# One tile fewer held as stored count blocks in passes 2 and 3 of a four-layer graph network kernel

## The chip, the cores and the metric

One NeuronCore of one Trainium2 chip runs the whole program. The metric is device time in microseconds (us) of one execution, the median of several runs.

## What is computed

A graph of 6250 nodes with 256 features and 106,250 directed edges (sources `src`, targets `dst`, sorted by target) goes through four layers, each followed by a residual sum and a layer norm. Cut to what matters here:

```python
# L0: weighted neighbour sums, two 256x256 products, row normalisation
# L1: three GIN layers on the unweighted graph:
agg = segment_sum(h[src], dst)            # the neighbour sum of each node
z = (1.0 + eps) * h + agg
h = relu(layer_norm(relu(z @ W1 + b1) @ W2 + b2 + h, gamma, beta))
# L2: degree-scaled neighbour sum, residual product, top-2 mixture of 64 experts, batch norm
# L3: weighted neighbour sums, one product
```

## The kernel before, in words

**Passes.** The nodes are 49 tiles of 128. Each of six neighbour sums is a *pass* over all 49 target tiles: pass 0 is L0, passes 1 to 3 are the GIN layers, pass 4 the sum of L2, pass 5 that of L3; the experts stand between passes 4 and 5. A pass's inputs are the outputs of the pass before, so little overlaps across its border.

**Two ways to sum.** In passes 1 to 4 a target tile is either *gathered* (sparse) or *held* (dense).
- A gathered tile has 18 chunks of 128 edges. For each chunk GpSimd issues one indirect DMA that fetches 128 rows of 512 floats, a value's high and low part (L2498), VectorE builds a 128x128 selection matrix (L3259), and TensorE multiplies the two (L2573, in pass 1 two halves at L2577).
- A held tile has 49 count blocks, 128x128 matrices of edge counts for each source tile, stored as bytes in `dense_blocks`. SyncE loads them in 7 parts (L2320), ScalarE widens them to float in 14 parts (L3085), and TensorE multiplies each with the source tile's rows that lie in SBUF (L2604, in pass 1 L2607).

**Building.** The blocks of 25 tiles (`DENSE`) are built in pass 0. Those of the tiles in `LATE` are built in pass 1, while it runs, for use from pass 2 on: for each of 13 places of a tile ScalarE and VectorE make one-hots (L3050, L3052, L3377), TensorE multiplies them (L2629), ScalarE copies the counts out as bytes (L3007) and SyncE stores them (L2268). Building needs the tile's edges sorted by source tile (`sort_into_bins`, VectorE L3282 to L3338). The other 24 tiles' edges are sorted too, for later passes: 14 in pass 1, one every 10 steps, and 10 in pass 3, one every 11 steps. With two tiles in `LATE`, passes 2 and 3 hold 27 tiles and gather 22. Pass 4 holds `DENSE` and one tile of `LATE`: 26 held and 23 gathered.

**Steps.** Every engine's program is written out at build time as a loop over steps `g`; six steps are one gathered tile, so a step is three chunks. `GROUPS[k]` is the number of gather steps of pass k: 144 in pass 1, 132 in passes 2 and 3, 138 in pass 4. The held tiles' blocks are spread evenly over the first `DSTEPS[k]` steps (120 in passes 2 and 3, 126 in pass 4), except that the first 28 blocks (`HEAD`) of a pass are multiplied at the end of the pass before. `_sequence` sets at which step each tile's sum is complete; the tile's layer work (operand, transposes, products, norm, split into parts, store) follows at fixed offsets from that step, on all engines (`OFFSETS`). Each engine works its program in order, so a late tile holds what stands behind it. GpSimd may run four steps ahead of TensorE (`RING`), VectorE's selection matrices two.

**Other work tied to steps.** In pass 2 a histogram of the edges' sources is taken, 49 parts, one every two steps from step 4 (`ONES_AT`): VectorE builds two large one-hot arrays (`one_hot`, L3451 to L3454) and TensorE multiplies them two steps later (`histogram`, L2707). A part's one-hots wait for the multiplication of the part before.

The change itself touches only the list at L1376; all schedules are computed from it.

Of the kernel before, what the change touches and what calls it, by code (L numbers as in the profile page):

```python
# [1372 lines left out]
DENSE_PASSES = (1, 2, 3, 4)  # L1373
WEIGHTED = {0: DENSE[1::3], 5: sorted(DENSE[1::2] + DENSE[4::8])}
EARLY_SPARSE = [t for t in range(NT) if t not in DENSE]
LATE = EARLY_SPARSE[6::12]  # L1376
LATE4 = LATE[:1]
HELD_IN = {1: DENSE, 2: sorted(DENSE + LATE), 3: sorted(DENSE + LATE), 4: sorted(DENSE + LATE4)}
STORED_AT = {t: i for i, t in enumerate(DENSE + LATE)}
NS = len(STORED_AT)  # L1380
# [10 lines left out]
SHORT = {0: 0, 1: 2, 2: 4, 3: 5, 4: 6, 5: 7, 6: 9, 8: 10, 9: 11}  # L1391
UNHELD = [t for t in EARLY_SPARSE if t not in LATE]
SORT_LATER = [t for pair in zip(LATE, UNHELD) for t in pair] + UNHELD[len(LATE):]
assert sorted(SORT_LATER) == EARLY_SPARSE
BINNED = [(0, t) for t in DENSE] + [(1 if j < SORTED1 else 3, t) for j, t in enumerate(SORT_LATER)]
BIN_AT = [APART * i for i in range(ND)] + [3 + SORT_APART[1] * i for i in range(SORTED1)] + [3 + SORT_APART[3] * i for i in range(NT - ND - SORTED1)]
BUILT = [(0, t) for t in DENSE] + [(1, t) for t in LATE] + [(5, t) for t in WEIGHTED[5]]
BIN_OF = [BINNED.index(b) if b in BINNED else None for b in BUILT]
# [2510 lines left out]
```

## Time and profile before

| | |
|---|---|
| runs | 5572.49, 5583.52 and 5602.99 us; median 5583.52 |
| span of the profiled execution, first to last instruction | 4918.0 us |
| what lies around the span, against the median | 665.5 us |
| mean granted TensorE clock | 0.947 |
| busy | TensorE 91%, VectorE 77%, GpSimd 65%, ScalarE 54% |

The profiled execution's own total is not listed, only its span; the difference to the median of the runs is what lies before the first and after the last instruction, and the spread between executions. "Busy" of TensorE is modelled from starts and contains short waits; VectorE's comes from recorded ends. A number like 4.26 us per step is worked out from the gathers counted in a window, three to a step.

### The profile page before, as it was taken

What the parts mean: (1) busy time and instruction counts of PE and PEld (TensorE: products, weight loads), DVE (VectorE), ACT (ScalarE), POOL (GpSimd) and SP (SyncE); (2) the same over time, 40 slices, a digit from 0 to 9 for tenths busy, and PEclk for the clock granted to TensorE, in tenths of its full rate; (3) what the DMA queues carried; (4) which work ended last, traced back from release to release, by engine and by line L of the source; (5) the groups of instructions that cost most, each with busy time, mean ns of one, the idle gap of its engine ahead of it and who ended that gap; (6) DMA issues with size and microseconds to landing.
All of it is one profiled execution on the core that took longest, in us unless ns stands there. A gap on an engine that the chain in (4) does not pass through costs nothing.

```text
span 4918.0 us, 84668 instructions
## 1 busy us (share of the span) xinstructions
PE 4481.9 (91%) x25759; PEld 3786.5 (77%) x25759; DVE 3796.1 (77%) x12081; ACT 2670.8 (54%) x6497; POOL 3216.8 (65%) x3227
## 2 busy tenths in 40 slices
PE   6999888889998899989999699996999877999998
PEld 4777777779997788857777488885999745888887
DVE  7888888759998799858988556667989457777776
ACT  4888888837553444535555344443555413454553
POOL 6777777767776666667666577672455363777776
PEclk9999999989999999989999899996999968999999
DMA  6444444488889888898888988885677533444443
GB/s 173 133 137 129 129 138 130 142 283 278 273 271 315 259 252 252 252 315 277 265 252 263 318 262 258 257 250 163 228 249 234 178 90 111 113 114 113 113 113 96
DMA packets 542065, 1005.46 MB, mean 204 GB/s; under 512 B 104266, under 2 KB 318920, under 8 KB 541324
## 3 DMA queue, kind: packets, MB, share of 16 engines
q0 software_dynamic: 206976, 637.24, 43.4%
q1 hardware_dynamic: 317354, 346.98, 21.6%
q10 hardware_dynamic: 17280, 15.74, 0.9%
q8 instruction: 217, 3.56, 0.3%
q14 instruction: 238, 1.95, 0.1%
HBM read 883.85 MB, written 117.06 MB: 204 GB/s over the span
## 4 chain that ended last, share of the span: by engine, by line
PE 43%; POOL 8%; issue 6%; DVE 5%; DMA 4%; ACT 1%; SPq 0%; ACTq 0%; POOLq 0%; DVEq 0%
PE PS L2604 15%; POOL ring L2498 5%; PE PS L2573 4%; PE PS L2862 4%; PE PS L2871 4%; PE PS L2756 4%; PE PS L2691 3%; PE PS L2580 2%; POOL more L2498 2%; PE PS L2741 1%; DMA ring<-expert_outputs,ring 1%; POOL slot_rows L2498 1%; PE PS L2730 1%; PE PS L2880 1%; POOL ring L2527 1%
## 5 line engine op out<-in xcount | busy, mean ns | idle before, releaser
L2498 POOL DMA_INDIRECT slot_rows<-planes,REC x1638 | 1580.3, 965 | 660.9 <-issue 433.6
L3085 ACT ACTIVATE wide_blocks<-HH 128x512 fp32r<-128x512 uint8 (+1 forms) x1470 | 831.7, 576 | 842.6 <-PE PS L2604 655.7
L2604 PE MATMUL PS<-plane_rows,wide_blocks 128*128 128x512 f32 x3920 | 1028.4, 409 | 17.2 <-ACT wide_blocks L3085 14.1
L2604 PEld LDWEIGHTS PS<-plane_rows,wide_blocks 128*128 128x128 f32 x3920 | 730.4, 192 | 173.3 <-ACT wide_blocks L3085 17.4
L2498 POOL DMA_INDIRECT ring<-in_x,REC x555 | 537.8, 969 | 210.8 <-issue 154.9
L2580 PE MATMUL PS<-ring,pick 128*128 128x256 f32 x2028 | 550.0, 404 | 60.2 <-DMA ring<-in_x,REC 32.6
L2498 POOL DMA_INDIRECT ring<-table,REC x459 | 442.7, 964 | 217.7 <-issue 208.5
L2691 PE MATMUL PS<-HH 128*128 128x256 f32 x2254 | 536.3, 379 | 0.0
L2580 PEld LDWEIGHTS PS<-ring,pick 128*128 128x128 f32 x2028 | 382.7, 200 | 158.1 <-DMA ring<-in_x,REC 48.8
L2691 PEld LDWEIGHTS PS<-HH 128*128 128x128 f32 x2254 | 413.9, 190 | 49.1
L2518 POOL DMA_INDIRECT ring<-second_outputs,ring x120 | 230.3, 1919 | 317.3 <-PE PS L2852 246.6
L3380 DVE TENSOR_SCALAR last_pass_pairs<-HH 128x256 fp32r<-128x256 f32 x780 | 278.1, 418 | 179.6 <-PE PS L2655 168.1
L2573 PE MATMUL PS<-slot_rows,slot_picks 128*128 128x512 f32 x1206 | 370.3, 410 | 49.2 <-DMA slot_rows<-planes,REC 46.8
L3259 DVE TENSOR_SCALAR slot_picks<-iotab,REC 128x128 fp32r<-128x128 bf16 x1638 | 376.5, 300 | 40.0 <-PE PS L2573 30.3
L2607 PE MATMUL PS<-plane_rows,wide_blocks 128*128 128x256 f32 (+1 forms) x2450 | 331.5, 289 | 6.0 <-DVE plane_rows L3668 6.0
L3257 DVE TENSOR_SCALAR pick<-iotab,REC 128x128 f32<-128x128 bf16 x1014 | 294.0, 352 | 41.8 <-PE PS L2580 39.1
L2573 PEld LDWEIGHTS PS<-slot_rows,slot_picks 128*128 128x128 f32 x1206 | 230.9, 192 | 123.2 <-DMA slot_rows<-planes,REC 45.5
L3050 ACT ACTIVATE last_pass_pairs<-iota,HH 128x128 fp32r<-128x128 f32 x390 | 135.1, 394 | 329.5 <-PE PS L2655 292.5
L2607 PEld LDWEIGHTS PS<-plane_rows,wide_blocks 128*128 128x128 f32 x2450 | 306.9, 192 | 8.0 <-DVE plane_rows L3668 6.2
L2966 ACT ACTIVATE TZT<-PS 128x256 f32<-128x256 f32 (+1 forms) x294 | 131.7, 448 | 250.0 <-PE PS L2730 248.3
L2756 PE MATMUL PS<-WA,TZT 128*128 128x256 f32 x980 | 247.3, 393 | 3.8 <-ACT TZT L2966 3.8
L2629 PE MATMUL PS<-HH 128*128 128x256 bf16 (+2 forms) x1075 | 223.1, 322 | 25.3 <-ACT HH L3011 19.8
(392 smaller groups left out, 9186.5 us busy)
## 6 DMA issues: line engine op xcount, KB each, us to landing
HH<-dense_blocks SPq DMA_DIRECT2D x735, 112.0 KB
HH<-in_L_gnn_w SPq DMA_DIRECT2D x128, 512.0 KB, 5.8
planes<-HN SPq DMA_DIRECT2D x188, 256.0 KB
plane_rows<-planes SPq DMA_DIRECT2D x57, 768.0 KB, 8.9
slot_rows<-planes,REC POOLq DMA_INDIRECT x1638
dense_blocks<-HH SPq DMA_DIRECT2D x25, 784.0 KB
expert_outputs<-ring ACTq DMA_DIRECT2D x120, 128.0 KB
ring<-in_x,REC POOLq DMA_INDIRECT x555
```

The source lines that it names most:

```text
L2498: pool.indirect_dma_start(to, None, planes[k] if dense else tables[k], bass.IndirectOffsetOnAxis(ap=at_rows, axis=0)).then_inc(s_slot[slot ...
L2518: pool.indirect_dma_start(XSB[c % MB], None, x2_dram, bass.IndirectOffsetOnAxis(ap=IDXC[:, c:c + 1], axis=0)).then_inc(s_xl[c % MB], 16)
L2573: last = mm(bank(j % 2, RP), slot_pick(k, slot), slot_row(k, slot, 0, RP), start=c == 0, stop=c == WT - 1)
L2580: last = mm(bank(j % 2, D), slot_pick(k, slot), slot_row(k, slot, 0, D), start=c == 0, stop=c == WT - 1)
L2604: last = mm(bank(5 + n % 2, RP), WIDE[:, at_block:at_block + P], plane(0, t, RP), start=t == 0, stop=t == NT - 1)
L2607: last = mm(bank(5 + n % 2, w), WIDE[:, at_block:at_block + P], plane(m, t, w), start=t == 0 and m == 0, stop=t == NT - 1 and m == 1, skip ...
L2691: last = mm(bank(sums_bank(v), D), AW32[f % OWN][:, s % 4 * P:(s % 4 + 1) * P], x_tile(SUMMED[v][0], s), start=pos == 0 and s == sources[0 ...
L2756: last = mm(bank(layer_bank(k), D), v, wmat(m, b), start=i == 0, stop=i == len(pairs) - 1)
L3085: fn(WIDE[:, e % XA * XW:e % XA * XW + w], AB[n % QA][:, lo:lo + w], ACT.Copy).then_inc(s_ax, 1)
L3257: last = v.tensor_scalar(p, iotab, lo, we, ALU.is_equal, ALU.mult)
L3259: last = v.tensor_scalar(p, iotab, lo, None, ALU.is_equal)
L3380: last = v.tensor_scalar(targets[fw % OWN][:, j * 2 * P:(j + 1) * 2 * P], iota1, BINS5[(u - NS) % 2][:, 0, c], BINS5[(u - NS) % 2][:, term ...
```

## The change

`LATE` is every twelfth tile of the tiles not in `DENSE`, from the seventh: tiles 12 and 38. It becomes the seventh alone, tile 12.

```diff
 EARLY_SPARSE = [t for t in range(NT) if t not in DENSE]
-LATE = EARLY_SPARSE[6::12]
+LATE = EARLY_SPARSE[6:7]
 LATE4 = LATE[:1]
 HELD_IN = {1: DENSE, 2: sorted(DENSE + LATE), 3: sorted(DENSE + LATE), 4: sorted(DENSE + LATE4)}
```

What follows from it by the planner: in pass 1 the blocks of tile 38 are not built or stored (its sort moves from pass 1 to pass 3 and tile 27's takes its place; still 14 and 10 sorts). In passes 2 and 3, 26 tiles are held and 23 gathered, so `GROUPS` is 138 in place of 132 and `DSTEPS` 126 in place of 120. Passes 0, 1, 4 and 5 keep their steps. The histogram and the sorts stay at the same step numbers.

## Rows read from the trace of the kernel before

**Rows 1.** The page: engines' busy time, and the granted clock in 40 slices.

```profile
PE 4481.9 (91%) x25759; PEld 3786.5 (77%) x25759; DVE 3796.1 (77%) x12081; ACT 2670.8 (54%) x6497; POOL 3216.8 (65%) x3227
...
PEclk9999999989999999989999899996999968999999
```

**Rows 2.** Busy by window (clock, DMA share, GB/s last), passes 1 to 4's gathers.

```profile
1036.00:1586.00 550.00, 523.85 (x4233) 508.39 (x4232) 490.22 (x1520) 290.96 (x687) 418.59 (x432) 0.97 0.89 279
1609.00:2157.00 548.00, 526.28 (x3230) 426.07 (x3229) 471.09 (x1164) 254.27 (x557) 382.97 (x396) 0.98 0.85 261
2182.00:2749.00 567.00, 518.97 (x2534) 421.75 (x2535) 472.84 (x1461) 307.58 (x735) 382.27 (x396) 0.96 0.86 271
2784.00:3338.00 554.00, 536.17 (x2642) 441.97 (x2642) 333.03 (x1406) 257.82 (x491) 394.09 (x414) 0.97 0.84 258
```

**Rows 3.** The same view: pass 1 with and without block building.

```profile
1130.00:1250.00 120.00, 118.33 (x1002) 115.73 (x1001) 112.63 (x361) 84.87 (x212) 91.34 (x95) 1.00 0.89 276
1300.00:1420.00 120.00, 119.58 (x999) 117.85 (x998) 111.67 (x344) 62.28 (x140) 91.34 (x95) 1.00 0.88 272
```

**Rows 4.** GpSimd's instructions in time, end of pass 1 and start of pass 2.

```profile
1584.30 0.95 POOL L2498 DMA_INDIRECT slot_rows<-planes,REC x1 [0.30 <-issue]
1585.56 0.94 POOL L2498 DMA_INDIRECT slot_rows<-planes,REC x1 [0.30 <-issue]
```

**Rows 5.** Busy by window: pass 2 in and after the histogram, pass 3's sorts.

```profile
1820.00:2040.00 220.00, 220.00 (x1461) 180.29 (x1460) 212.84 (x499) 109.17 (x239) 150.15 (x155) 1.00 0.83 250
2050.00:2100.00 50.00, 50.00 (x259) 41.44 (x258) 32.06 (x99) 25.65 (x56) 35.11 (x37) 1.00 0.85 259
2250.00:2700.00 450.00, 424.85 (x2118) 348.63 (x2117) 396.73 (x1210) 258.65 (x625) 293.51 (x304) 0.98 0.84 262
```

**Rows 6.** The chain by line, 1820 to 2040 us; its TensorE counts from groups by line.

```profile
by line: PE PS L2604 59.2%; PE PS L2573 16.4%; PE PS L2741 8.7%; PE PS L2756 8.1%; PE PS L2707 5.7%; PE PS L2730 2.0%
...
L2604 PE MATMUL PS<-plane_rows,wide_blocks 128*128 128x512 f32 x558 | 143.9, 405 | 0.0
```

**Rows 7.** Waits of the engines, 1820 to 2040 us (total, times, longest).

```profile
POOL slot_rows L2498 <- PE PS L2573: 36.3, 44, 1.7
...
PEld PS L2707 <- DVE HH L3454: 0.8, 3, 0.3
```

**Rows 8.** VectorE groups by line, 1820 to 2040 us.

```profile
L3453 DVE TENSOR_TENSOR HH<-LANES,PS 128x2304 bf16<-128x2304 bf16 x26 | 66.4, 2554 | 0.9
L3259 DVE TENSOR_SCALAR slot_picks<-iotab,REC 128x128 fp32r<-128x128 bf16 x156 | 36.3, 305 | 0.1
L3454 DVE TENSOR_TENSOR HH<-LANES,PS 128x882 bf16<-128x882 bf16 x26 | 27.7, 1066 | 0.0
L3540 DVE SCALAR_TENSOR_TENSOR TZ<-plane_rows,EPS,PS 128x256 f32<-128x256 f32 x21 | 10.0, 476 | 0.3
...
L3511 DVE BATCH_NORM_STATS2 ST<-TU 128x6 f32<-128x256 f32 x20 | 8.6, 428 | 0.7
...
L3512 DVE BATCH_NORM_AGGREGATE MV<-ST 128x2 f32<-128x6 f32 x20 | 3.6, 182 | 0.7
L3598 DVE RECIPROCAL SM<-SM 128x1 f32<-128x1 f32 x20 | 3.1, 154 | 0.0
```

**Rows 9.** Waits of the engines in pass 3's sorts, 2250 to 2700 us.

```profile
DVE HN L3437 <- ACT HN L2989: 15.4, 8, 3.7
PE PS L2730 <- DVE TZ L3543: 14.8, 9, 4.0
...
DVE SM L3519 <- ACT SM L2948: 9.8, 7, 3.0
...
PE PS L2756 <- ACT TM L2973: 7.3, 4, 2.4
...
DVE TU L3580 <- ACT HN L2989: 5.4, 5, 2.9
```

**Rows 10.** GpSimd groups, pass 2's histogram and pass 4.

```profile
L2498 POOL DMA_INDIRECT slot_rows<-planes,REC x155 | 150.6, 971 | 70.2 <-PE PS L2573 36.3 <-issue 33.8
...
L2498 POOL DMA_INDIRECT slot_rows<-planes,REC x149 | 141.7, 951 | 59.6 <-issue 39.5 <-PE PS L2573 20.1
```

**Rows 11.** TensorE and ScalarE groups of block building, pass 1.

```profile
L2629 PE MATMUL PS<-HH 128*128 128x256 bf16 (+1 forms) x50 | 9.8, 271 | 0.0
...
L3052 ACT ACTIVATE HH<-HH,ones 128x256 bf16<-128x256 bf16 x26 | 13.2, 509 | 0.8
```

## The prediction

> **What bounds the kernel now.** I read the page's busy shares first: TensorE is the busiest engine over the whole program [rows 1], but an average does not price an edit in three passes. So the next view is busy time by window, one window per pass from its first gather to its last [rows 2]. The change touches passes 1, 2 and 3; pass 4 already has the mix of 26 held and 23 gathered tiles. The reader should take the gather counts from these rows: three gathers are a step. Pass 1 takes 550/144 = 3.82 us per step, pass 2 548/132 = 4.15, pass 3 567/132 = 4.30, pass 4 554/138 = 4.01.
>
> Pass 1 is held by GpSimd. Its gathers stand back to back, 0.95 us each and 0.30 us of issue [rows 4], so 1.25 us per gather and 3.76 us per step; 432 of them need 541 of the 550 us.
>
> Passes 2 and 3 are not. In pass 2's histogram stretch 155 gathers, 51.7 steps, take 220 us: 4.26 us per step. There TensorE is busy 220 of 220 us, and VectorE 212.8 [rows 5]. The waits say who is late: GpSimd waits for TensorE's products, and TensorE for VectorE only 0.8 us [rows 7]. But no VectorE wait of any size stands in that stretch either; what is left between its busy time and 220 us is small gaps between dependent instructions. So **two engines are full at once**, each with about 4.26 us of work per step, and relief of one of them is worth only what the other allows. After the histogram (2050 to 2100 us) VectorE falls to 32 of 50 us, TensorE stays full, and a step takes 50/12.3 = 4.05 us [rows 5].
>
> In pass 3's stretch of sorts (304 gathers, 101.3 steps, 450 us) a step takes 4.44 us, and nobody is full: TensorE waits 14.8 us for VectorE's operands and 7.3 for ScalarE, some 25 us in all; VectorE waits 15.4, 9.8 and 5.4 us for ScalarE, some 32 in all [rows 5, 9]. Work per step is then (450-25)/101.3 = 4.20 us for TensorE and (450-32)/101.3 = 4.13 for VectorE; they cost each other 0.24 us per step more than the fuller one needs.
>
> **Pass 1.** Thirteen places of block building go. By the rows of both tiles together [rows 11] it is half of 9.8 us of TensorE, half of 13.2 us for one of ScalarE's three kinds of instruction, and 26 VectorE one-hots; SyncE loses 13 stores. The cover is the gathers: in 120 us with building and in 120 us without, GpSimd issued 95 gathers each time [rows 3]. So the pace does not see this work, and I take 0. The bounds: at most the 9 us that pass 1 takes over its back-to-back gathers can be won; nothing can be lost, since sorts and steps stay as many. Were GpSimd faster, TensorE (524 of 550 us) would be next.
>
> **Passes 2 and 3, per step.** Before, 27x49-28 = 1295 blocks in 120 steps are 10.79 per step; after, 26x49-28 = 1246 in 126 steps are 9.89. Tiles that come due per step go from 27/120+1/6 = 0.392 to 26/126+1/6 = 0.373.
> - TensorE: one block is 59.2% of 220 us over 558 = 0.233 us; a tile's layer work is (8.7+8.1+2.0)% of 220 us over 20 tiles = 2.07 us [rows 6]. Each step gets 0.90x0.233+0.019x2.07 = 0.25 us shorter: 4.26 to 4.01 with histogram. The histogram's 5.7% is 0.24 per step; without it 3.77.
> - VectorE: 26 histogram parts per 52 steps and 3 selection matrices per step stay. The 12 groups of a tile's layer work, of which four are shown (L3540 to L3598), sum to 91.2 us for 20 tiles, 4.6 us per tile [rows 8]. So a step gets only 0.019x4.6 = 0.09 us shorter: 4.26 to 4.17.
> - GpSimd: unchanged at 3.76, in practice the 3.82 of pass 1. ScalarE and SyncE do less (14 widenings and 7 loads fewer per pass). 18 gathers more per pass are also 18 slots of the DMA queues; each moves 128x2 KB, 4.7 MB against 0.8 MB of blocks saved, 4 MB at 261 GB/s [rows 2] over a pass of 143 MB: the DMA share stays near 0.85.
>
> **Pass 2, the sum.** The histogram stands at fixed step numbers and covers 98 steps. After the change VectorE is the fuller engine there, so 98 x (4.17-4.26) = -8. The 16 further steps with blocks go from 4.05 to GpSimd's 3.82: -4. Six steps are added, at 3.82: +23. Sum **+11 us**.
>
> **Pass 3, the sum.** In the sorts' 101 steps TensorE's work falls from 4.20 to 3.95, VectorE's from 4.13 to 4.02 (5.6 us per tile, an estimate: this pass has a second norm, so 4.6 plus once more L3511 and L3512, 0.43 and 0.18, two reciprocal-like steps of 0.15 as L3598, and a little [rows 8]). With the same loss of 0.24 over the fuller engine, which is now VectorE, a step takes 4.27 in place of 4.44: -17. Some six steps with blocks after the sorts: -1. Six added steps: +23. Sum **+5 us**. No row shows how the two engines' clashes go when VectorE is the fuller one. Bounds: the loss vanishes (4.02, -42, hence -20 for the pass), or the pace stays at 4.44 (0, hence +22). The value taken is nearest to the row of that stretch itself.
>
> The borders of the passes keep their form: what is waited for there is the last tiles' chain, whose offsets do not change, and 0 is booked for it.
>
> Total: 0+11+5 = **+16 us** on the profiled span of 4918.0 us, 4934. The 665.5 us between the span and the median are taken as unchanged, so 5583.5+16 = **5600 us**, +0.3%.
>
> **A rule weighed.** GpSimd's issue takes 971 ns on average beside the histogram's VectorE work and 951 ns in pass 4 [rows 10]: 0.06 us per step, in both cases below the pace of the fuller engine. The Trainium skill, SBUF — State Buffer, section SBUF: two separate sides, says that a DMA issued by GpSimd can be locked out while VectorE runs an operation in a two-port mode, since descriptors go through a shared port. That speaks against this change, which adds gathers beside a full VectorE. By that rule a gather could wait out a whole 2.55 us instruction; the trace shows 20 ns more on the mean, so the sum goes by the row.
>
> **Rivals.**
> - *TensorE alone sets the pace* (VectorE's fullness is coincidence and hides in its lead of two steps). Then pass 2's histogram steps take 4.01: 98 x (-0.25) -4 +23 = -5; pass 3: 101 x (-0.25) -1 +23 = -3. Total -8, 5575 us. For: TensorE has no idle time in 1820 to 2040, and waits for VectorE 0.8 us. Against: VectorE has none either, and even a full lead of two steps, 8 us, is used up after 50 of the 98 steps at 0.16 us per step. Chance 0.18.
> - *Slower: the steps keep their pace.* Place: the chain from VectorE's operand through transposes, ScalarE's copies and norms and back, in both stretches. If that chain, and not either engine's total, sets the pace, fewer blocks between its links shorten nothing: pass 2 0 -4 +23 = +19, pass 3 0 -1 +23 = +22, total +41, 5624 us, over the bound. It decides once the wait for operands grows by as much as the blocks shrink, 0.25 us per step. For: pass 3's 32 us of VectorE waits on ScalarE. Against: pass 2 shows hardly any. Chance 0.17.
> - *Pass 1 gives its 9 us back* with TensorE's pace in the others: 5566 us. Against: the 95 and 95 gathers. Chance 0.05.
> - The clock: in pass 3's sorts the granted clock is 0.98, behind waits of up to 4 us, and 1.00 in pass 2's full stretch [rows 5, 9]; that is the higher level, 2.4 GHz, with short falls to 1.2. If pass 2 falls to 0.98 it loses under 1% of TensorE's 4.01 us, inside VectorE's slack. No case of its own.
> - That the change does not do what it says is ruled out by the planner's own lists, which give 138 steps.
>
> **How the numbers follow.** The forecast has 0.60. The range reaches from the second rival's 5575 with a few us for pass 1, 5569, to just under the slower rival's value, 5622; about 0.2 lies outside. About 0.5% (28 us) is what a measurement of this kernel can tell from no change. Faster by more needs more than the pass 1 rival: 0.03. Slower by more: most of the slower rival's 0.17 and a tail of the forecast, 0.19. Within: 0.78.
>
> **What would show it.** In the changed profile: 414 gathers in passes 2 and 3; in pass 1 the same 550 us and half of L2629's count. In pass 2's histogram stretch 4.17 us per step, VectorE still full, TensorE waiting for VectorE (L2707 for L3454, or L2730 for the operand) by some 0.16 us per step, and GpSimd's waits no larger; 4.01 per step would show the first rival, 4.26 the second. After the histogram GpSimd back to back at 3.8. Pass 2 as a whole 559 us, pass 3 572. The prediction is wrong if pass 2 gets shorter, or if a border of passes changes by more than a few us.

## The result, and the profile after

The change made the kernel 0.27% slower: 5605.3 us against 5590.1 us, medians of 20 executions of each on one chip, ratio 1.0027 (95% interval 1.0017 to 1.0038), some +15 us. One of the 20 after the change took 8667 us at a granted clock of 0.50, and the ratio leaves it out. The forecast was +16 us and "no change within 0.5%". So the size held. How it comes about did not hold in all its steps, and one assumption underneath it was plainly wrong.

The page of the kernel after: span, busy time by engine, and the granted clock in 40 slices.

```profile
span 5599.5 us, 84379 instructions
...
PE 4659.7 (83%) x25669; PEld 3884.2 (69%) x25669; DVE 3808.1 (68%) x12089; ACT 2606.3 (47%) x6417; POOL 3231.6 (58%) x3263
...
PEclk8999989989999899997999899997899968999999
```

**The profile before was not typical.** The span after is 5599.5 us and that execution took 5601.1 us: only 1.6 us lie around the span (2.4 us in the second profile of before). The prediction took the 665.5 us between the span of before (4918.0) and the median as time outside the span. They were inside it: the profiled execution of before was some 12% quicker than any that was timed ("the quick execution" below). A second profile of the unchanged kernel (first experiment, "the second profile of before") spans 5584.1 us. From here on the comparison is with that one. Its busy sums are nearly those of [rows 1], with idle time between them:

```profile
span 5584.1 us, 84668 instructions
...
PE 4678.6 (84%) x25759; PEld 3899.6 (70%) x25759; DVE 3803.1 (68%) x12081; ACT 2637.4 (47%) x6497; POOL 3196.7 (57%) x3227
```

Busy time by window in the second profile of before (window, length, the five engines with their instruction counts, then granted clock, DMA share, GB/s). The rows are: pass 1, pass 2, two stretches of pass 2 (in and after the histogram), pass 3, two stretches of it (in and after the sorts), pass 4. The long ones answer to [rows 2], the stretches to [rows 5].

```profile
1183.00:1856.00 673.00, 567.29 (x4229) 538.10 (x4230) 488.55 (x1513) 283.31 (x687) 413.71 (x432) 0.93 0.76 230
1882.00:2551.00 669.00, 563.46 (x3227) 446.24 (x3225) 472.74 (x1163) 246.33 (x555) 379.84 (x396) 0.93 0.72 216
1920.00:2360.00 440.00, 382.48 (x2325) 304.18 (x2326) 339.06 (x789) 171.87 (x386) 238.88 (x249) 0.94 0.68 200
2460.00:2540.00 80.00, 64.13 (x286) 50.93 (x285) 43.77 (x143) 26.78 (x65) 51.69 (x55) 0.89 0.86 280
2575.00:3188.00 613.00, 535.76 (x2537) 425.75 (x2538) 473.53 (x1464) 302.53 (x733) 380.19 (x396) 0.95 0.82 252
2643.00:3093.00 450.00, 410.11 (x2004) 327.25 (x2003) 374.12 (x1158) 240.30 (x586) 275.54 (x286) 0.98 0.81 247
3105.00:3180.00 75.00, 57.20 (x252) 44.85 (x251) 48.88 (x163) 29.41 (x76) 45.69 (x48) 0.84 0.85 281
3221.00:3858.00 637.00, 561.94 (x2643) 448.56 (x2642) 330.35 (x1387) 245.45 (x485) 392.72 (x414) 0.95 0.75 225
```

The same view of the kernel after, the same eight places:

```profile
1178.00:1848.00 670.00, 563.42 (x4199) 534.05 (x4197) 483.20 (x1479) 260.13 (x633) 413.00 (x432) 0.93 0.77 231
1874.00:2546.00 672.00, 563.48 (x3194) 443.66 (x3194) 475.93 (x1181) 241.81 (x540) 396.18 (x414) 0.92 0.74 221
1920.00:2360.00 440.00, 378.55 (x2331) 300.88 (x2330) 347.23 (x809) 165.69 (x371) 247.08 (x259) 0.94 0.70 205
2440.00:2540.00 100.00, 78.77 (x342) 60.50 (x340) 56.09 (x185) 32.46 (x77) 65.86 (x68) 0.89 0.85 277
2570.00:3199.00 629.00, 536.40 (x2512) 420.64 (x2512) 482.00 (x1495) 297.58 (x720) 398.18 (x414) 0.94 0.81 253
2638.00:3088.00 450.00, 402.44 (x1941) 317.51 (x1942) 378.51 (x1162) 232.09 (x563) 283.47 (x295) 0.97 0.81 249
3100.00:3190.00 90.00, 67.61 (x297) 52.73 (x297) 56.25 (x193) 38.25 (x98) 57.12 (x59) 0.91 0.86 286
3231.00:3870.00 639.00, 559.53 (x2636) 448.18 (x2636) 330.97 (x1387) 245.73 (x485) 392.21 (x414) 0.95 0.75 224
```

Read the gather counts at the end of each row, three to a step. In 440 us of the histogram there are 249 before and 259 after: 5.30 and 5.10 us per step. In 450 us of the sorts there are 286 and 295: 4.72 and 4.58. After the histogram a step takes 80/(55/3) = 4.36 and 100/(68/3) = 4.41 us, after the sorts 4.69 and 4.58. Then the lengths: pass 1 673 and 670, pass 2 669 and 672, pass 3 613 and 629, pass 4 637 and 639. The added time is in the passes the prediction named, more of it in pass 3 than in pass 2 here.

Read also the engines' own columns. In the histogram stretch TensorE is busy 382 of 440 us and VectorE 339. Neither is full, unlike in [rows 5]. That is what the experiments had to explain.

### The profile page after: what moved, and what is told of

Its sections match the earlier page's. It is cut to its first block, busy times and chain, and to the rows that moved or that the text cites. A ratio compares the mean times of both kernels' runs of the same rounds, so it can differ in the third digit from the quotient of the medians.

```text
span 5599.5 us, 84379 instructions
## 1 busy us (share of the span) xinstructions
PE 4659.7 (83%) x25669; PEld 3884.2 (69%) x25669; DVE 3808.1 (68%) x12089; ACT 2606.3 (47%) x6417; POOL 3231.6 (58%) x3263
## 4 chain that ended last, share of the span: by engine, by line
PE 42%; another core or an unknown queue 8%; issue 6%; DVE 5%; ACT 3%; DMA 1%; POOL 1%; SPq 0%; ACTq 0%; DVEq 0%; POOLq 0%
PE PS L2604 14%; PE PS L2862 4%; PE PS L2573 4%; PE PS L2871 4%; PE PS L2691 4%; PE PS L2756 3%; PE PS L2580 3%; ACT wide_blocks L3085 2%; PE PS L2655 1%; PE PS L2741 1%; DVE last_pass_pairs L3380 1%; PE PS L2730 1%; PE PS L2880 1%; DMA slot_rows<-planes,REC 1%
## 5 line engine op out<-in xcount | busy, mean ns | idle before, releaser
L2498 POOL DMA_INDIRECT slot_rows<-planes,REC x1674 | 1603.0, 958 | 1024.6 <-issue 425.4
L3085 ACT ACTIVATE wide_blocks<-HH 128x512 fp32r<-128x512 uint8 (+1 forms) x1442 | 793.2, 573 | 1145.8 <-PE PS L2604 483.1
L2604 PE MATMUL PS<-plane_rows,wide_blocks 128*128 128x512 f32 x3822 | 1066.1, 422 | 177.0 <-ACT wide_blocks L3085 147.9
L2604 PEld LDWEIGHTS PS<-plane_rows,wide_blocks 128*128 128x128 f32 x3822 | 726.0, 198 | 377.6 <-ACT wide_blocks L3085 174.0
L2691 PE MATMUL PS<-HH 128*128 128x256 f32 x2254 | 561.6, 392 | 8.6 <-issue 4.4
L2580 PEld LDWEIGHTS PS<-ring,pick 128*128 128x128 f32 x2028 | 403.3, 207 | 132.9 <-issue 47.1
L2691 PEld LDWEIGHTS PS<-HH 128*128 128x128 f32 x2254 | 430.5, 197 | 66.3 <-issue 6.3
L2573 PE MATMUL PS<-slot_rows,slot_picks 128*128 128x512 f32 x1242 | 391.3, 423 | 40.1 <-DMA slot_rows<-planes,REC 34.6
L2607 PE MATMUL PS<-plane_rows,wide_blocks 128*128 128x256 f32 (+1 forms) x2450 | 360.0, 300 | 64.2 <-ACT wide_blocks L3085 38.0
L2756 PE MATMUL PS<-WA,TZT 128*128 128x256 f32 x980 | 268.9, 418 | 70.1 <-issue 41.1
L2756 PEld LDWEIGHTS PS<-WA,TZT 128*128 128x128 f32 x980 | 200.2, 210 | 115.0 <-issue 49.0
```

The lines of the kernel that those rows point to most:

```text
L2498: pool.indirect_dma_start(to, None, planes[k] if dense else tables[k], bass.IndirectOffsetOnAxis(ap=at_rows, axis=0)).then_inc(s_slot[slot ...
L2573: last = mm(bank(j % 2, RP), slot_pick(k, slot), slot_row(k, slot, 0, RP), start=c == 0, stop=c == WT - 1)
L2580: last = mm(bank(j % 2, D), slot_pick(k, slot), slot_row(k, slot, 0, D), start=c == 0, stop=c == WT - 1)
L2604: last = mm(bank(5 + n % 2, RP), WIDE[:, at_block:at_block + P], plane(0, t, RP), start=t == 0, stop=t == NT - 1)
L2607: last = mm(bank(5 + n % 2, w), WIDE[:, at_block:at_block + P], plane(m, t, w), start=t == 0 and m == 0, stop=t == NT - 1 and m == 1, skip ...
L2691: last = mm(bank(sums_bank(v), D), AW32[f % OWN][:, s % 4 * P:(s % 4 + 1) * P], x_tile(SUMMED[v][0], s), start=pos == 0 and s == sources[0 ...
```

## The experiments

Ratios are to the kernel before, executed beside it on the same chip. Profiles of one kernel differ: pass 4, with no edit in it, took from 631.3 us (nohot_after) to 640.6 us (p3_only) by the gathers' starts, so a single pass length decides only what is larger than some 9 us. Where no interval is given, the time is that of a single execution.

### Is the first profile typical? (c_before)

The kernel before, unchanged.

> The kernel before, unchanged, for a second profile. The profiled execution of before had a span of 4918 us where the timed runs take about 5590; that of after has 5600 us, and each of its listed spans is 1.6 us below its time. Theory A: the earlier profile of before caught an unusually quick execution, and 665 us never lay around the span; then this span is about 5588 us and pass 1 takes some 4.65 us per step instead of 3.82, as in after. Theory B: the two kernels differ that much inside the span; then it is near 4920 again.

Measured: 5586.5 us, span 5584.1. The first profile was a quick execution; there is no time of 665 us outside the span. Whether a rare execution, another chip or another way of recording made it quick, no run here tells. A stretch of the timeline shows the kind of place where the time goes (start, duration, instruction, and in brackets the engine's idle time before it and what is taken to have ended it):

```profile
1253.44 1.23 PE L2619 MATMUL PS<-HH 128*128 128x130 bf16 x18
...
1254.48 2.17 PE L2607 MATMUL PS<-plane_rows,wide_blocks 128*128 128x256 f32 x16
...
1257.67 0.95 POOL L2498 DMA_INDIRECT slot_rows<-planes,REC  x1 [0.30 <-issue]
1260.01 0.24 DVE L3332 TENSOR_REDUCE HH<-PS 128x26 f32<-128x78 f32 x1 [5.10 <-remote]
1260.11 1.56 ACT L3085 ACTIVATE wide_blocks<-HH 128x512 fp32r<-128x512 uint8 x3 [7.14 <-remote]
...
1260.79 0.51 PE L2607 MATMUL PS<-plane_rows,wide_blocks 128*128 128x256 f32 x2 [4.14 <-ACT wide_blocks L3085]
...
1262.60 0.95 POOL L2498 DMA_INDIRECT slot_rows<-planes,REC  x1 [3.98 <-PE PS L2577]
```

TensorE's last block product ends at 1256.65 us. The widening on ScalarE needs the buffer that TensorE frees, and starts at 1260.11, 3.5 us later, three widenings at once. VectorE, which reads what TensorE made at 1254.67 (L2619), starts at 1260.01 as well. TensorE then waits for the widening, GpSimd for TensorE. So signals of TensorE seem to reach the other engines some us late. TensorE's ends are modelled from the starts, so the widening alone would leave open that the last product really ended late. VectorE speaks against that: 16 further products had started behind L2619 by then. "remote" in brackets says only that no releaser was found: this profile holds 39,419 records of semaphore updates where the first held 96,343, so here the name of a releaser is weaker evidence than in [rows 7].

Who waits in the histogram stretch of this profile (1920 to 2360 us; total, times, longest), to be held against [rows 7]:

```profile
POOL slot_rows L2498 <- PE PS L2573: 137.6, 61, 5.7
ACT wide_blocks L3085 <- PE PS L2604: 122.2, 93, 5.4
ACT wide_blocks L3085 <- remote: 85.3, 17, 7.0
...
DVE PS L3451 <- remote: 59.0, 22, 5.7
PEld PS L2604 <- ACT wide_blocks L3085: 57.1, 20, 4.7
PE PS L2604 <- ACT wide_blocks L3085: 50.6, 21, 4.3
...
DVE PS L3451 <- PE PS L2707: 16.2, 10, 3.0
```

GpSimd, ScalarE and VectorE all wait for TensorE here, VectorE for the histogram's products of the part before (L3451, 75 us by both rows), while TensorE waits for ScalarE's widening.

### Does pass 1 give anything back? (build_only)

Passes 2 and 3 as after the change; tile 38 is still built and stored in pass 1.

```diff
-HELD_IN = {1: DENSE, 2: sorted(DENSE + LATE), 3: sorted(DENSE + LATE), 4: sorted(DENSE + LATE4)}
+HELD_IN = {1: DENSE, 2: sorted(DENSE + LATE4), 3: sorted(DENSE + LATE4), 4: sorted(DENSE + LATE4)}
```

> Tile 38 is still built and stored in pass 1, but gathered in passes 2 and 3 (26 held, 23 gathered): the pass 1 part of the change is undone. My theory (pass 1 is paced by GpSimd, building is covered): same time as after, ratio to before 1.003. Rival (building costs pass 1 up to 9 us): ratio 1.0045, some 9 us above after.

Measured: 5616.7 us, 1.0045 (1.0024 to 1.0065), an interval that overlaps that of the change. Its pass 1, from first gather to last, is 670.9 us, against 669.9 without the building and 672.1 before; its passes 2 and 3 are 671.3 and 626.8 us. That profile is of the quickest of its seven executions (5583.1 us), 34 us below their median, so its pass 1 is weak evidence. The timed ratio is the rival's own, 1.0045. By the two ratios not building saves 0.0018, 10 us, but with their half-widths of 0.0021 and 0.0011 this doesn't stand apart from nothing. All profiles with three buffers of widened blocks say little rather than nothing: pass 1 takes 669.0 to 671.8 us in the three with one tile built and 670.9 to 675.9 us in the six with two, 3 us less on the mean.

### One pass alone (p2_only, p3_only)

As build_only, but with `sorted(DENSE + LATE4)` in entry 2 alone, and in entry 3 alone.

> Only pass 2 holds 26 and gathers 23; pass 3 stays at 27 and 22; both tiles built. My theory: VectorE's histogram keeps pass 2 from gaining, +11 us, ratio 1.002. Rival TensorE alone: -5 us, ratio 0.999. Rival pace kept: +19 us, ratio 1.0035.

> Only pass 3 holds 26 and gathers 23; pass 2 stays at 27 and 22; both tiles built. My theory: +5 us, ratio 1.001. Rival TensorE alone: -3 us, ratio 0.9995. Rival pace kept: +22 us, ratio 1.004.

Measured: pass 2 alone 5593.0 us, 1.0014 (1.0001 to 1.0027); pass 3 alone 5593.1 us, 1.0013 (1.0001 to 1.0025); before 5586.5. Each is +7 to +8 us, and with both tiles built the two add up to the whole, which leaves nothing for pass 1. The two ratios expected, 1.002 and 1.001, lie inside these intervals; those of both rivals lie outside, TensorE alone (0.999 and 0.9995) only just. The timed runs don't tell the passes apart. By the profiles, the mean of pass 2 with 26 held tiles (after, build_only, p2_only: 672.0, 671.3, 671.8) less that with 27 (second profile of before, p3_only: 668.2, 661.5) is +7 us, and of pass 3 (628.5, 626.8, 634.4 less 613.2, 618.0) +14 us.

### Is VectorE the fuller engine? (nohot_before, nohot_after)

The large one-hot arrays of the histogram are made for the first of its 49 parts only, before and after the change. The other parts' high one-hots, products and waits stay.

```diff
-                v.tensor_tensor(OHL, LANES1.unsqueeze(1).broadcast_to((P, HCH, P)), SLOP.unsqueeze(2).broadcast_to((P, HCH, P)), ALU.is_equal)
+                if g == 0:
+                    v.tensor_tensor(OHL, LANES1.unsqueeze(1).broadcast_to((P, HCH, P)), SLOP.unsqueeze(2).broadcast_to((P, HCH, P)), ALU.is_equal)
```

> The kernel before, with the large one-hot instruction of the histogram (L3453, 2.55 us) only for the first of its 49 parts; the others multiply the first part's one-hots again. Left out: 48 of the 49 large one-hot arrays, so the out-degrees are not those of the graph. VectorE sheds 48 x 2.47 = 119 us in pass 2. If VectorE is what holds pass 2 at 5.06 us per step in the second profile of before (theory), pass 2 falls from 668 us by some 30 us or more, with the other passes unchanged. If TensorE and its chain with ScalarE hold it (rival), pass 2 keeps 660 to 668 us.

> The same omission in the kernel after. Theory: with VectorE relieved, pass 2 is held by TensorE's work, of which the change removes 0.25 us per step, so pass 2 comes out 5 us shorter than in nohot_before, where with the histogram whole it was 4 us longer (672 against 668). Rival: what the change does to pass 2 does not depend on the histogram; again about 4 us longer.

Measured: 5571.3 us, 0.9986 (0.9971 to 1.0001), and with the change 5593.9 us, 1.0025 (1.0008 to 1.0042). The histogram stretch of nohot_before:

```profile
1920.00:2360.00 440.00, 391.99 (x2411) 310.59 (x2410) 247.82 (x770) 174.49 (x390) 246.80 (x258) 0.95 0.70 207
```

VectorE is busy 91 us less than in the second profile of before, 4.09 less 2.88 = 1.2 us per step, and a step gets shorter from 5.30 to 5.12 us. So of what VectorE is relieved of, 15% comes back as pace. It may be less: p3_only, whose pass 2 is that of before, did 255 gathers in the same stretch, 5.18 us per step. Nor did relief turn the change into a gain in pass 2: its length goes from 655.8 to 671.5 us, +16; the theory had -5, the rival +4. VectorE's total is not what sets the pace of pass 2.

### Is TensorE's work the pace? (half_dense)

The block products are 256 wide in place of 512, except for the first and last source tile; the low parts of the other 47 source tiles' rows are left out of the sums.

```diff
-last = mm(bank(5 + n % 2, RP), WIDE[:, at_block:at_block + P], plane(0, t, RP), start=t == 0, stop=t == NT - 1)
+last = mm(bank(5 + n % 2, D if 0 < t < NT - 1 else RP), WIDE[:, at_block:at_block + P], plane(0, t, D if 0 < t < NT - 1 else RP), start=t == 0, stop=t == NT - 1)
```

> The kernel before, with the multiplications of the held tiles' blocks in passes 2 to 4 only 256 columns wide for 47 of 49 source tiles. Left out: the low parts of the rows in the held tiles' sums. TensorE sheds about 0.11 us per block, some 1.2 us per step of passes 2 and 3. If TensorE's work sets the pace (theory now), pass 2 falls from 668 us by 80 us or more and pass 3 from 613 likewise. If the pace is set by waits that do not depend on how long TensorE works (rival: signals that reach the other engines late), they fall by less than 30 us each.

Measured, in a single execution: 5573.1 us beside 5593.4, where the nine of before lie between 5573.2 and 5609.5, so no gain clear of the spread. Pass 2 takes 662.4 us and pass 3 610.7, 6 and 2.5 us less than in the second profile of before, as the rival has it. The histogram stretch, and L2604 by line over the program (count, busy, mean ns, idle before):

```profile
1920.00:2360.00 440.00, 318.20 (x2330) 273.24 (x2329) 337.35 (x785) 163.62 (x382) 241.08 (x251) 0.85 0.68 203
```

```profile
L2604 PE MATMUL PS<-plane_rows,wide_blocks 128*128 128x256 f32 (+1 forms) x3920 | 735.5, 332 | 353.7 <-ACT wide_blocks L3085 249.9
```

TensorE sheds 64 us in the stretch and does 251 gathers' worth of steps where before there were 249: 5.26 us per step. What it sheds it now spends waiting for ScalarE's widening (249.9 us over the program, against 135.3 in the second profile of before, shown below). So TensorE's total isn't the pace either. The granted clock is lower in this emptier stretch, 0.85 against 0.94; that may be why TensorE sheds 0.8 us per step (4.61 to 3.80) and not the 1.2 expected.

### The loop through the widened blocks (xa4)

One more buffer between ScalarE's widening and TensorE's block products.

```diff
-XA = 3
+XA = 4
```

> The kernel before, with four buffers of widened blocks in place of three, so that TensorE may run about 14 blocks, not 10, on what ScalarE has widened. In the second profile of before TensorE waits 65 us for ScalarE's widening in pass 2. If that loop with three buffers is what lets late signals through to TensorE (theory), passes 1 to 4 get shorter by 20 us or more each, ratio 0.98 or below. If the late signals hit all engines alike (rival), the ratio is above 0.995.

Measured: 5499.9 us, 0.9837 (0.9818 to 0.9856), 1.6% faster. In the second profile of before, who waited for the widening, by its line:

```profile
L3085 ACT ACTIVATE wide_blocks<-HH x1470: 503/572/637, 1163.6 to 3815.3; 128x512 fp32r<-128x512 uint8 x184
...
  PE PS L2604: 494.0, 350
  remote: 308.3, 115
...
  PE PS L2604: 135.3, 80
```

The same in xa4:

```profile
L3085 ACT ACTIVATE wide_blocks<-HH x1470: 504/572/636, 1165.8 to 3734.4; 128x512 fp32r<-128x512 uint8 x184
...
  PE PS L2604: 291.9, 237
  remote: 185.9, 76
...
  PE PS L2604: 58.9, 33
```

and its histogram stretch:

```profile
1920.00:2360.00 440.00, 405.68 (x2602) 322.89 (x2601) 374.19 (x871) 188.88 (x425) 265.93 (x278) 0.98 0.74 223
```

The first two figures under each heading are ScalarE's idle time before a widening, the last TensorE's wait for one: 135 us fall to 59. A step of the histogram takes 4.75 us in place of 5.30, pass 2 614.3 us in place of 668.2. The other passes gain less than the 20 us expected of each: pass 1 takes 666.4 us for 672.1, pass 3 598.6 for 613.2, pass 4 625.2 for 636.2. No work was taken away, only a fourth block part may be on its way while TensorE's release is late. So in pass 2 the round trip from TensorE to ScalarE and back through three buffers holds the pace in good part. In the quick execution it didn't show: there TensorE's idle time before L2604 was 0.0 us in the stretch of [rows 6].

### More and fewer held tiles (three, five, none23)

`LATE` with three and with five tiles, held in passes 2 and 3 (28 held and 21 gathered, 30 and 19); and with none of them held in these passes (25 and 24).

```diff
-LATE = EARLY_SPARSE[6::12]
+LATE = EARLY_SPARSE[6::6]
```

```diff
-LATE = EARLY_SPARSE[6::12]
+LATE = EARLY_SPARSE[4::4]
```

```diff
-LATE = EARLY_SPARSE[6::12]
+LATE = EARLY_SPARSE[6:7]
-HELD_IN = {1: DENSE, 2: sorted(DENSE + LATE), 3: sorted(DENSE + LATE), 4: sorted(DENSE + LATE4)}
+HELD_IN = {1: DENSE, 2: DENSE, 3: DENSE, 4: sorted(DENSE + LATE4)}
```

> One tile more instead of one less: tiles 12, 24 (or its neighbour) and 38 built in pass 1, 28 held and 21 gathered in passes 2 and 3, pass 4 unchanged. If the change's sign holds on both sides (theory: a held tile costs less than a gathered one as long as VectorE has work tied to steps), 126 steps give about 4 us less in pass 2 and 10 us less in pass 3, ratio 0.998. If before was at the optimum (rival: with 11.7 blocks per step TensorE is the bound), the ratio is 1.000 to 1.005.

> Five tiles of blocks built in pass 1 (30 held, 19 gathered in passes 2 and 3, 114 steps). With three the time was 21 us below before; each tile from 26 to 27 to 28 took 5 to 20 us off a pass. Theory: the slope goes on but flattens as blocks per step rise from 11.2 to 13.2 and TensorE's work per step from 4.4 to 4.8 us: ratio 0.992, pass 2 about 625 us, pass 3 about 605. Rival: TensorE's bound is met and pass 1 pays for five builds: ratio 0.996 to 1.000.

> The kernel after with pass 2 and 3 at 25 held and 24 gathered (tile 12 is built and held for pass 4 alone): the change's part in passes 2 and 3 once more. Theory: each further gathered tile adds 5 to 15 us to a pass, so pass 2 680 us and pass 3 640 us, against 672 and 628 after. Rival, TensorE's relief catches up once steps are light: pass 2 and 3 no longer than after.

Measured, with the passes from first gather to last:

| held in passes 2 and 3 | steps | time, us | before beside it | ratio | pass 1 | pass 2 | pass 3 |
|---|---|---|---|---|---|---|---|
| 25 (none23, executed once) | 144 | 5637.9 | 5580.7 | 1.010 | 671.8 | 678.9 | 656.6 |
| 26 (after) | 138 | 5605.3 | 5590.1 | 1.0027 | 669.9 | 672.0 | 628.5 |
| 27 (second profile of before) | 132 | | | 1 | 672.1 | 668.2 | 613.2 |
| 28 (three) | 126 | 5559.7 | 5580.7 | 0.9960 (0.9947 to 0.9974) | 674.9 | 641.0 | 611.0 |
| 30 (five) | 114 | 5508.6 | 5593.4 | 0.9856 (0.9835 to 0.9878) | 676.7 | 591.3 | 605.4 |

A held tile is the cheaper kind all along, by 19 to 35 us each in passes 2 and 3 together, and building three more makes pass 1 5 us longer in these profiles, no more than an untouched pass moves. The change went one step up a slope that goes on in both directions. The expectations had the sign and not the size: three was put at 0.998 with 4 and 10 us in passes 2 and 3 (27 and 2 came), five at 0.992. The histogram stretch of five shows what the shorter way fills:

```profile
1920.00:2360.00 440.00, 428.18 (x2625) 344.61 (x2625) 353.95 (x832) 215.15 (x477) 235.09 (x246) 0.99 0.72 210
```

246 gathers in 440 us, 5.37 us per step, little more than before with 27 tiles, although a step now carries (30x49-28)/102 = 14.1 blocks in place of 10.8 (the blocks are spread over all steps but the last 12). TensorE is busy 428 of 440 us. The added blocks went into its idle time: over the whole program it waits 70 us for the widening, where before it was 135. To the other side it is different: none23 does 272 gathers in the same stretch, 4.85 us per step with 9.1 blocks, so there a step does get lighter with its blocks, by 0.25 us from the 26 held tiles of after.

### The two together (xa4_five)

Both edits, `XA = 4` and `LATE = EARLY_SPARSE[4::4]`.

> Both edits that helped, together: four buffers of widened blocks and five tiles built in pass 1 (30 held, 19 gathered in passes 2 and 3). Alone they gave 0.984 and 0.986. If each acts on its own term, the one on TensorE's waits for ScalarE's widening and the other on the number of steps, they add up: ratio 0.970 to 0.975. Rival: both take away the same waits, so together they give little more than the better one: ratio 0.980 to 0.984.

Measured: 5405.5 us beside 5519.7 for the kernel before on that chip, 0.9786 (0.9762 to 0.9809). The best of all, but less than the two gains added (1.6 and 1.4%). The interval lies above the 0.970 to 0.975 of the theory and reaches the rival's 0.980 to 0.984 at its upper end. Its histogram stretch fits the rival's reason: TensorE is full again, 437 of 440 us at full clock.

```profile
1920.00:2360.00 440.00, 437.18 (x2746) 358.23 (x2743) 372.26 (x879) 226.13 (x494) 244.50 (x254) 1.00 0.75 220
```

Both edits draw on the same idle time of TensorE, and in this stretch it is used up.

## Why the prediction was right, and where it was not

**Right: the size and the sign.** +16 us forecast, +15 measured, inside the bound of 0.5%. It rested on two things. The runs bear out that the six added steps in each pass cost more than the removed blocks give back. That pass 1 gives nothing is right within a few us: the profiles give it 3 us on the mean, the ratio of build_only allows 10, that of p2_only and p3_only none.

**The base was wrong.** "The 665.5 us between the span and the median are taken as unchanged" treated as outside what was inside. The passes expected at 559 and 572 us came out at 672 and 629. The difference survived because it was worked out per step, and both of its terms came out somewhat larger than put, in opposite directions:

| term | as predicted | as the stretches show |
|---|---|---|
| pass 2, a histogram step | 4.26 to 4.17, x98 = -8 | 5.30 to 5.10, x98 = -20 |
| pass 2, the 16 steps after it | -4 | +0.05 x16 = +1 |
| pass 2, six added steps | x3.82 = +23 | x4.41 = +26 |
| pass 3, a sort step | 4.44 to 4.27, x101 = -17 | 4.72 to 4.58, x101 = -14 |
| pass 3, six steps after | -1 | -0.11 x6 = -1 |
| pass 3, six added steps | x3.82 = +23 | x4.58 = +27 |
| sum | +16 | +19 |

By these terms pass 2 gets +7 and pass 3 +12 us, close to the profiles' means (+7 and +14); +11 and +5 were forecast. The sum of +19 against +15 measured is within what one profile's stretches can tell.

The split can be had more firmly from the starts of all gathers, in the two profiles with 27 held tiles and the three with 26 (c_before, after, build_only, p2_only, p3_only). In pass 2 the first 104 steps get 17 us shorter and the rest, with six steps more, 24 us longer. In pass 3 the first 116 get 12 us shorter and the rest 26 us longer. The forecast had -8 and +19, and -17 and +22. So it saved too little in pass 2, too much in pass 3, and put the added steps too cheap. That these errors nearly cancel to the measured +15 is luck; what was sound is that each pass weighs six added steps against lighter ones.

The sum of the prediction also leaves out the steps with blocks before the stretch of sorts: it counts 101 and 6 of the 120. At its own 0.17 us that is 2 us. And 98 x 0.09 is 8.8, not 8.

**The step that failed: "after the change VectorE is the fuller engine there".** The whole reading "two engines are full at once" was true of the one quick execution, and no other profile shows it. In typical ones both have idle time in the histogram. The sign named for it, TensorE waiting 0.16 us per step for VectorE, stayed away: in the 440 us of the kernel after, L2707 waits 0.6 us for L3454, and GpSimd 121.6 us for TensorE's products.

```profile
POOL slot_rows L2498 <- PE PS L2573: 121.6, 58, 4.6
...
PEld PS L2707 <- DVE HH L3454: 0.6, 1, 0.6
```

Taking 1.2 us per step from VectorE gave back 0.18 us per step, halving the block products 0.04, and a fourth buffer for widened blocks, which takes no work away, 0.55. By the first of these rates the 0.09 us that the change takes from VectorE would be worth 0.01 us, not the 0.20 seen (0.17 on the mean of the five profiles). That the 0.20 us come through the block loop, which 0.9 blocks per step fewer pass, is argued and not shown: with fewer (none23) a step got 0.25 us lighter again, but with more (three, five) only 0.07 us longer, so the loop has no fixed price per block. One rival has no run at all: VectorE's one-hots of a part wait for TensorE's product of the part before, 75 us in this stretch, and no kernel had a second buffer there. With the large one-hots left out these waits only grew, to 105 us (L3451, 71.9 and 32.7), so the late side there is TensorE's product, not the one-hots.

**"An added step costs 3.82".** That was GpSimd's back-to-back pace in the quick execution. In typical ones a step behind the histogram or the sorts takes 4.4 to 4.7 us, and one of a pass's last 12, which carry no blocks, still 4.2 to 4.5. GpSimd's own rate isn't to blame: where the gathers stand back to back, they are 1.25 us apart in both profiles, as in [rows 4]. The rest is waiting, for buffers that TensorE releases among others (as the 3.98 us in the timeline above).

**Rivals.** TensorE alone (-8 us, 5575, ratio 0.9986) falls by the interval of the change and by half_dense, though its 0.25 us per step was nearer to the 0.20 seen in pass 2 than the forecast's 0.09. "The steps keep their pace" (+41, 5624, ratio 1.0073) falls by the same interval and by the gather counts, 259 for 249 and 295 for 286, though its place, a chain between engines rather than an engine's total, was the better picture. It was sought in the layer work; the one that a run could shorten is the block loop. The pass 1 rival's total (5566) falls with TensorE's pace; its 9 us in pass 1 are three times what the profiles show.

**The rule weighed** went as the row said. In the histogram stretch a gather's issue takes 238.88/249 = 0.959 us in the second profile of before. With the large one-hots left out it takes 246.80/258 = 0.957 us. The Trainium skill (SBUF — State Buffer, section SBUF: two separate sides) ties the lockout of a GpSimd-issued DMA to VectorE operations in a two-port mode. No row here shows that L3453 ran in one; it took 2554 ns for 2304 elements in a row. So the prediction's "wait out a whole 2.55 us instruction" had no ground in the rows. The trace shows no such wait in the issue times, and it doesn't test the rule.

**Open.** Why TensorE's signals are late in typical executions and were not in the first one isn't settled. The block products' spacing (L2604, median 0.234 and 0.235 us) and that of gathers back to back (1.25 us) are the same in both, the busy sums nearly; the granted clock is lower (0.916 to 0.947), but that may be a result of the waits. None of the later executions was of the quick kind, so nothing could be tried on it. One thing goes with the late restarts: ScalarE's waits marked "remote" before a widening are 115 (308 us) in the second profile of before, 146 (429 us) in half_dense, 57 (156 us) in five and 52 (103 us) in xa4_five, rarer the fuller TensorE is. Whether TensorE's idle time makes them or they make it stays open, and with it why more blocks per step cost so little.

## What to carry to other kernels

Before costing an edit from a profile, hold its span against the timed executions: if they differ by more than a few us, the profile may be of another kind of execution, and its full engines may not be full in the ones that are timed. Where two engines look equally full, look for the buffers between them; one more buffer may be worth more than any shift of work. And where two ways of doing a tile compete, try the split one step to the other side too: here the measured slope pointed the other way from the change, and three more held tiles with one buffer more gave 2.1%.

## What the runs showed of the hardware

- The same program ran once in 4918.0 us under the profiler, while its timed executions took from 5558 to 5609 us (5510 to 5543 on the chip of xa4_five). Busy sums differed by up to 4.4% (TensorE 4482 and 4679 us); the rest is idle time between instructions. The quick profile holds 96,343 records of semaphore updates, the 13 others 37,671 to 42,335, so it may also have been recorded in another way.
- In the typical executions several engines start again together some us after TensorE, by its modelled ends, has done what they need, as in the timeline above (3.5 and 5.3 us). In pass 2 of the second profile of before the widening alone has 25 waits marked "remote", 110.9 us in sum and 7.0 at most.
- Half the width for 3760 of 3920 block products changed the time by 0.4% in a single execution, within the spread of before (5573.2 to 5609.5 us).
